# Attention: the order of scores, side work and value products within a step of TensorE's program

## The reference

```python
S, R, DH = (8, 2, 16)
sq = (x @ wq_s).reshape(b, n, S, DH).transpose(0, 2, 1, 3) * scale
sk = (x @ wk_s).reshape(b, n, S, DH).transpose(0, 2, 1, 3)
rv = (x @ wv_r).reshape(b, n, R, DH).transpose(0, 2, 1, 3)
search_sim = jnp.einsum('bsid,bsjd->bsij', sq, sk)
search_attn = jax.nn.softmax(search_sim, axis=-1)
retrieved = jnp.einsum('bsij,brjd->bsird', search_attn, rv)
...
retrieval_attn = jax.nn.softmax(retrieval_sim, axis=-1)
out = jnp.einsum('bsir,bsird->bsid', retrieval_attn, retrieved)
```

## Time and profile before

| | us |
|---|---|
| median of 3 runs | 5733.49 |
| lowest and highest run | 5732.6, 5741.53 |
| the profiled execution (span) | 5736.7 |
| of it the attention's steps, from 1570 to 3938 | 2368 |

### The profile page before, as it was taken

How to read it: one execution, slowest core, us unless ns; L and a number is a source line. 1 busy time by engine, 2 the same in 40 slices (tenths; PEclk the granted TensorE clock), 3 DMA queues, 4 the chain that set the end, 5 groups by cost and what they waited for, 6 DMA issues and landing times. The chain is left out here.

```text
span 5736.7 us, 63937 instructions
## 1 busy us (share of the span) xinstructions
PE 4699.7 (82%) x19695; PEld 1764.3 (31%) x19695; DVE 3076.5 (54%) x5438; ACT 1975.9 (34%) x2773; POOL 633.7 (11%) x882
## 2 busy tenths in 40 slices
PE   4599999947699898888888888896699999855423
PEld 2233333315122222222222222223344444443212
DVE  4777777748666666556555555553300000357663
ACT  3211111127044444444444444455343434412200
POOL 1000000007101111111110110014100000201201
PEclk9799999979599999999999999998899999966655
DMA  1344444427411112222122222201000000112404
GB/s 63 79 103 91 92 99 92 95 82 262 66 21 19 19 21 27 27 27 27 23 27 27 27 27 27 27 5 50 29 0 0 0 0 0 54 64 80 122 0 128
DMA packets 173099, 290.74 MB, mean 51 GB/s; under 512 B 23207, under 2 KB 98989, under 8 KB 171453
## 3 DMA queue, kind: packets, MB, share of 16 engines
q1 hardware_dynamic: 144696, 252.65, 20.8%
q10 hardware_dynamic: 23808, 25.17, 1.2%
q0 software_dynamic: 4368, 10.07, 0.6%
HBM read 92.39 MB, written 67.63 MB: 28 GB/s over the span
## 5 line engine op out<-in xcount | busy, mean ns | idle before, releaser
L1474 DVE TENSOR_REDUCE at_mx<-at_side 128x1 f32<-128x512 f32 x2048 | 1336.6, 687 | 452.2 <-PE at_side L1387 445.8
L1543 ACT ACTIVATE at_P<-at_S 128x1024 f32<-128x1024 f32 x1024 | 997.1, 1024 | 1345.6 <-PE at_S L1412 1281.0
L1422 PE MATMUL at_pv<-at_P,at_rvb 128*64 128x512 f32 x4096 | 1113.1, 627 | 71.6 <-issue 54.1
L1387 PE MATMUL at_side<-at_ko,at_qo 96*128 96x512 bf16 x2048 | 757.7, 400 | 63.2 <-DMA at_ko<-qk 38.0
L1412 PE MATMUL at_S<-at_qo,at_ko 99*128 99x512 bf16 x2048 | 594.9, 381 | 22.6 <-DMA at_qo<-at_mrow 22.3
L1784 PE MATMUL ff_ph<-ffn_Y,ff_w 128*128 (+1 forms) x1024 | 525.5, 595 | 9.3 <-DMA ff_b<-in_b_dram 9.3
L1814 ACT ACTIVATE ff_hs<-ff_ph,ff_b 128x512 f32<-128x512 f32 x512 | 351.7, 687 | 525.3 <-PE ff_ph L1784 525.3
L1798 PE MATMUL ff_po<-ff_hs,ff_w2s 128*128 128x512 f32 x1024 | 523.2, 593 | 0.0
L616 PE MATMUL la_acc<-la_rep,la_wagg 128*32 128x512 f32 x4096 | 511.2, 606 | 1.1 <-DMA la_rep<-la_pad 1.1
L773 DVE SCALAR_TENSOR_TENSOR la_dwq<-la_pad,la_taps,la_dwq 128x1024 f32<-128x1024 f32 x384 | 491.7, 1280 | 7.2
L1833 DVE SCALAR_TENSOR_TENSOR X<-ff_po,ffn_b2w,X 128x512 f32 (+1 forms) x32 | 24.0, 751 | 823.8 <-PE ff_po L1798 823.8
(11 more groups left out here) (410 smaller groups left out, 4194.6 us busy)
## 6 DMA issues: line engine op xcount, KB each, us to landing
la_rep<-la_pad SPq DMA_DIRECT2D x512, 162.2 KB, 3.6
qk<-ap_part SPq DMA_DIRECT2D x32, 768.0 KB, 3.7
at_qo<-qk SPq DMA_DIRECT2D x96, 256.0 KB, 9.8
at_ko<-qk SPq DMA_DIRECT2D x96, 256.0 KB, 20.1
n_ln_xs<-X SPq DMA_DIRECT2D x96, 256.0 KB, 2.3
X<-in_x_dram SPq DMA_DIRECT2D x4, 2048.0 KB, 22.2
proj<-la_y POOLq DMA_DIRECT2D x32, 256.0 KB, 2.3
lan_y<-proj SPq DMA_DIRECT2D x8, 1024.0 KB, 5.0
```

The source lines that it names most:

```text
L1387: return pe.matmul(side[bank][:, :], qo[1 - u][0:KQ, s, i * C:(i + 1) * C], ko[1 - u][0:KQ, s, h * CH:(h + 1) * CH], start=True, stop=True)
L1422: last = pe.matmul(pv_acc[hp][64 * i:64 * i + 64, :], rvb[u][:, j, :], P[k % 2][:, 2 * hp + i, :], start=(j == 0), stop=(j == 7))
L1474: v.reduce_max(mx[:, n // 2, n % 2:n % 2 + 1], side[bank][:, :], AX.X).then_inc(side_saved, 1)
L1543: a.activation(P[k % 2][:, 2 * hp:2 * hp + 2, :], S[hp][:, :, :], ACT.Exp).then_inc(p_ready, 1)
```

## The change

The four parts become three. The side work is cut in thirds, each at the head of a part. Behind the first third come the scores of pair 0 (of step k + 2), behind the second those of pair 1, and after the last third the value products of both pairs. Of five fills two stand at the head, one between the scores and two before the values; a single fill (tokens, rows) stands between the scores, of six there are two in each part. In step 30 and 31 both score pairs of the next image stand at the head. The programs of the other engines are the same.

```diff
-                        for part in range(4):
-                            for w in work[(part * len(work) + 2) // 4:((part + 1) * len(work) + 2) // 4]:
+                        for part in range(3):
+                            for w in work[(part * len(work) + 1) // 3:((part + 1) * len(work) + 1) // 3]:
                                 fill(w, b, u, side_base(b) + at, (u + 1 + at) % 2).then_inc(side_ready, 1)
                                 at += 1
-                            if part < 2:
-                                values(b, u, k, part)
-                            elif k + 2 < STEPS:
-                                scores(b, u, k + 2, part - 2)
-                            elif not last and part == 2:
+                            if part < 2 and k + 2 < STEPS:
+                                scores(b, u, k + 2, part)
+                            elif part == 0 and not last:
                                 lead(b + 1, 1 - u, k + 2 - STEPS)
+                        for hp in range(2):
+                            values(b, u, k, hp)
```

## The result

| | before | after |
|---|---|---|
| median, us | 5733.92 | 6199.23 |
| lowest and highest run | 5732.6, 5741.53 | 6196.92, 6204.06 |
| span of the profiled execution | 5736.7 | 6202.5 |
| attention's steps, in the trace | 2368 | 2839 |

The account below looks back on a forecast made before the run. TensorE was taken to bound the attention, busy 2147 of 2368 us. Longer steps sum to 502 us, less 66 at load waits and 6 at branch pauses: 5733.5 + 430, rounded to 6165 us, range 6060 to 6270 (80%).

Parts of the forecast that it names:

- the sum: Attention slots: 421 us for 14 middle ones, 33 first, 48 last, together 502; less 66 and 6, +430 us.
- Who waits for whom: Attention steps: exponentials wait for the previous step's value products, scores for exponentials; value products queue behind the scores on TensorE.
- The steps: Attention step times: plain +0.80 us, without fills +1.67, token fill only +0.98, token and five max fills +0.57.
- The scores of the next image: Step 30: they wait for row data 5.3 us after the row fill; the step takes 5.2 us against 4.14.
- A step with the copies: Steps 0, 8, 16, 24: ScalarE copies the finished group out of PSUM before its exponential, adding 0.96 us each.
- The gain of the batch: Steps with fills: one switch less (0.09 us) and value products in a row (0.17), at most 0.26 us.
- The first rival: Exponentials end before scores are reached, only 0.26 us gained in 390 steps: -101 us, 5632 us; chance 4%.
- What is given back: Wait for loads at k = 3: falls from 12.6 to about 5.3 us, nine times, -66 us.
- The pause at the branch: Loop branch, five slots: some 13.6 us, length kept; ScalarE's copy and exponential run partly under it, -6 us in all.
- my terms: Forecast added time per attention slot: 30.1 us in a middle slot, 33 in the first, 48 in the last.
- The second rival: Steps without fills drop to 1.2 GHz, +2.3 us each, +120 to +244 us: 6285 to 6410 us; chance 9%.
- The third rival: Waits for loads and pauses at the branch vanish, the longer slot hiding loads and code: 6049 us; chance 6%.

## Why the prediction was right

It said 6165 us within 6060 and 6270, and measured are 6199.23: 465 us more than before, where the sum had 430. The mechanism was the forecast one; that nine of the slots came out to 0.1 us is luck (below). Point by point:

- **Who waits for whom** was right: exponentials behind the value products, scores behind the exponentials, value products never waiting. Handing P over pair by pair takes 176 us away again, with TensorE's program in the changed order.
- **The steps.** Plain 4.98 forecast, 5.00 measured; without fills 4.51 and 4.57; token only 4.56 and 4.51; token and five fills 5.61 and 5.59. The scores of the next image start 5.26 us after the row fill (2256.52 to 2261.78), forecast 5.3. A step with the copies is 5.97 (value products at 2370.72 and 2376.69), which is the 0.96 that I added.
- **The gain of the batch**, at most 0.26 a step, is not shown by itself in any run: 0.03 came of it where the exponentials still bind, and 0.30, more than the bound, in token steps where the token's place changed too. The first rival gave this gain to every step with fills once the exponentials are out of the way, and 5632 us. The batch at the head of the step is that case, and it takes 5880. The rival had left out that the drains lose their cover.
- **What is given back.** The loads end 32.4 us after the row fill (2443.98 to 2476.41), forecast 32.5. But I had the wait at 5.3 us nine times, 48 in all, and it was 12.4 in eight rows. TensorE arrived later than steps at the full clock would have it.
- **The pause at the branch** kept its length, as I had taken it: 14.36 against 13.6.

**The term that was missed** is the clock, which the sum put at nothing. In the five slots with the pause the change costs 170.4 us (934.7 against 764.3), so 34.1 each, where my terms give 30.1 - 1.2 = 28.9. That is 26 us over, and what the value batches of these slots take over 1.94 is 24.2; the kernel with the extra matmuls brings these slots to 182.0 on average, that is 29.2 over before. In the nine others it costs 204.5, 22.7 each, forecast 22.8, by luck: there the same slow steps eat the wait for the loads, which I had too long. The first slot, row fill to row fill (127.9 to 163.1), is 35.1 longer where the terms give 29 (33 less steps 29 to 31), and its first three batches account for 4.1 of the 6. From the last row fill to the last value product it is 107.9 before and 168.5 after, 60.6 where the terms give 3.9 for the end of that slot and 48 for the last one: 9 over, with 8.6 in slow batches. Together the slots are 40 us over the terms and the rest of the kernel is 5 under, which makes the 35. The second rival had the mechanism, but not its size: it let the steps without fills run at 1.2 GHz because they are 69% busy, for 120 to 244 us. In the last slot most of them held 2.4 GHz at 67%, and six batches of its steps from 8 on did not, for 8.2 us. Most of what fell stood behind the rows, the copies and the branch.

The third rival, the pauses gone altogether, was wrong in half: the waits for loads nearly went, those at the branch stayed.

## What to carry to other kernels

Between two engines that hand buffers back and forth, look at what lies in TensorE's queue between the release of a buffer and the next instruction that needs it back: here 1.87 us of ready value products had stood over the 1.94 us of a step's exponentials, and the change moved them out from between. Side work in few buffers wants to be spread over the step in proportion to the time that its consumer needs, not packed where it looks tidy; a batch that saves 0.3 us of TensorE can cost more in drains. And a wait for something that ends at a fixed time absorbs gains and losses ahead of it alike, so price a change slot by slot, not by the sum of its steps alone.

## What the runs showed that I had not expected

- Six drains of some 0.63 us each (3.12 for five) fit in a step of 4.71 us or take 5.03, by nothing but the places of their fills among four parts (2, 2, 1, 1 or 2, 1, 2, 1): 88 us of the kernel.
- The pause at the loop's branch is some 13.6 us while the twelve transfers of 256 KB with the operands are under way, and 2.6 to 3.4 us in the two kernels where they start after it.
- Most steps at 67% busy keep the full clock in this kernel, but a few neighbours with the same pauses (1.19 and 0.31 us) do not. The slow batches, there and behind pauses of 2.4 us and more, took 2.4 to 3.7 us instead of 1.94.
